# All three convolutions of a conv block as sixteen 32x32 TensorE tiles in two alternating image layouts, with halo rows copied by DMA, one ring of eight PSUM banks, and 16-bit quantising

## The chip, the cores and the metric

The kernel runs on one core of a Trainium2 chip. The metric is the device time of one execution in microseconds, from the first to the last instruction of the slowest core and what little lies around them; lower is better. TensorE is called PE here, VectorE DVE, ScalarE ACT, GpSimd POOL and SyncE SP, as in the profile.

## What is computed

```python
x = x + conv0(gn(x))          # x: 8 images x 32 channels x 128 x 128, f32
x = x + disco(gn(x))          # the output

def conv0(v):                 # 3x3, 32 -> 32 channels, quantised per tensor
    qx = clip(round(v * (127 / max|v|)))      # max over all 8 images
    qw = clip(round(w * (127 / max|w|)))
    return conv3x3(qx, qw) * (max|v| * max|w| / 127**2) + bias

def disco(v):                 # two 3x3 convolutions whose corner taps are zero
    h = lrelu(instnorm(conv5(v, w1)), 0.2)
    return lrelu(instnorm(conv5(h, w2)), 0.2)
```

`gn` is a group normalisation (16 groups of two channels), `instnorm` normalises each channel of each image. The 3x3 kernels of `conv5` are summed from 36 given planes; only the middle and its four neighbours are not zero, so it has five taps where `conv0` has nine. The convolutions are named 0, 1 and 2 below; conv 0 is in f16, conv 1 and 2 are in f32.

## The kernel before

**Layout.** An image stands in SBUF as 128 partitions x 4096 columns. The four groups of 32 partitions are the four parities (row even or odd, column even or odd) of the pixels of each channel, so a group holds a 64x64 image, and a tap either stays in a group or reads another group at a shift of one. Input and output come in this layout by the host's reshaping. The eight images, 2 MB each, stay in `xs` for the whole kernel.

**Matmuls.** One PSUM bank holds 512 columns: eight rows of 64 for all four parities. Convs 1 and 2 use tiles of 64x32: 64 input partitions, 32 output ones, eight tiles of the array (`half_taps`, lines 980 and 986), 32 matmuls for two banks. Conv 0 uses 128x32 tiles (line 1039) for images 0 to 2, and 64x32 ones (`taps0`, lines 1057 and 1064) from image 3 on, which need a copy of the image with its upper and lower partitions exchanged (`qturn`, by DMA, line 304). An image and convolution is four units of two banks. PSUM is a ring of three units (`SLOTS`), and two banks for the small gathers.

**The prologue.** SP loads the images two at a time. DVE and ACT take the statistics of every image, POOL writes the normalised one (line 586), DVE takes its maximum (line 762), and POOL reduces the maxima over the partitions (line 601). Then scale and shift of the quantising are known for all images (line 799, `quant_known`).

**The main part.** Every engine's order is written out by hand, and semaphores connect them. PE goes through `ORDER`: (0,0), (0,1), then for t = 0 to 5 conv 1 of image t, conv 0 of t+2, conv 2 of t, and at last (1,6), (1,7), (2,6), (2,7). What follows a unit:

- conv 0: DVE adds the scaled sum onto x in `xs` (`x1_unit`, line 811) and takes statistics of that (line 817); POOL makes scale and shift of them (`normalise`, lines 554 to 566), ACT writes the normalised image (`make_a`, line 409), the input of conv 1.
- conv 1 and 2: DVE takes statistics in PSUM (`conv_stats`, line 827), ACT copies the unit out (`take`, line 396), and after POOL's `normalise` ACT applies the leaky ReLU (`make_h`, line 419, or `norm_out`, line 428). DVE adds the result of conv 2 and the bias onto x (`output`, line 844), and SP stores it (line 312).
- POOL quantises image t+3 in pieces (`quantise`): scale and shift to f32 (line 634), + 12582912 (line 637), - 12582912 to f16 (line 642).

In each normalisation a matmul of 128x128 on PE (`gather`, line 944) sums the statistics over the partitions that belong together, between DVE's `spread` and `group_moments`.

Of the kernel before, what the change touches and what calls it, by code (L numbers as in the profile page):

```python
# [8 lines left out]
I32 = mybir.dt.int32  # L9
# [8 lines left out]
BLK = IMG // 2  # L18
COLS = BLK * BLK
PAD = BLK + 2  # L20
BANK = 512
BANKS = COLS // BANK
ROWS = BANK // BLK
UNITS = 4
UBANKS = 2
UCOLS = UBANKS * BANK
UROWS = UBANKS * ROWS
SLOTS = 3
EDGES = [0, UROWS + 1, 2 * UROWS + 1, 3 * UROWS + 1, BLK]
QCOLS = (UROWS + 1) * BLK  # L30
TAPS = 9
# [4 lines left out]
KEEP_Q, KEEP_A, KEEP_H = 40, 60, 60  # L36
# [9 lines left out]
GN_ORDER = [0, 1, 2, 3, 4, 5, 6, 7]  # L46

# [36 lines left out]
def conv_block_kernel(nc, x_d, w0_d, bias_d, w12_d, const_d, out_d):  # L84
    psi = disco_psi()
    with ExitStack() as ctx:
# [3 lines left out]
        def sem(name):  # L90
# [3 lines left out]

        xs = sb("xs", [P, B * COLS], F32)
        apad = [sb(f"apad{p}", [P, PAD, PAD], F32) for p in range(2)]
        hpad = sb("hpad", [P, PAD, PAD], F32)
        qpad = sb("qpad", [P, PAD, PAD], F16)
        qturn = sb("qturn", [P, PAD, PAD], F16)
        scaled = sb("scaled", [P, QCOLS], F32)  # L100


        q_one = apad[1][:].rearrange("p r c -> p (r c)").bitcast(F16)[:, 0:PAD * PAD].rearrange("p (r c) -> p r c", c=PAD)
        h_last = xs[:, 0:PAD * PAD].rearrange("p (r c) -> p r c", c=PAD)
        a_last = xs[:, 2 * COLS:2 * COLS + PAD * PAD].rearrange("p (r c) -> p r c", c=PAD)
        own0 = sb("own0", [P, 2, 2, C], F16)
        side0 = sb("side0", [P, 2, 2, C], F16)
        vert0 = sb("vert0", [P, 2, 2, C], F16)
        corn0 = sb("corn0", [P, 2, 2, C], F16)
        turn0 = sb("turn0", [P, 2, 2, C], F16)  # L110
        own12 = sb("own12", [P, 2, 2, 2, C], F32)
        side12 = sb("side12", [P, 2, 2, 2, C], F32)
        vert12 = sb("vert12", [P, 2, 2, 2, C], F32)
        const = sb("const", [P, 2 * P + 3 * (GN_MEMBERS + IN_MEMBERS)], F32)
        single = sb("single", [P, 11], F32)
        bias, minus_half, wmax, wmax_all, wmul, amax1, sx, sx_inv, qmul, dequant, centre = (
            single[:, n:n + 1] for n in range(11))
# [18 lines left out]
        kern = scaled[0:C, 0:2 * TAPS * C].rearrange("p (v k o) -> p v k o", v=2, k=TAPS)  # L136
        kern0 = scaled[0:C, 2 * TAPS * C:].bitcast(F16)[:, 0:TAPS * C].rearrange("p (k o) -> p k o", o=C)
# [5 lines left out]


        stage_at = (B - 1) * COLS

        def staged(cols):
            nonlocal stage_at
            v = xs[:, stage_at:stage_at + cols]
# [3 lines left out]
        w0 = staged(TAPS * C)[0:C]  # L153
        w0_s = staged(TAPS * C)[0:C]
# [3 lines left out]
        gathered_gn = ctx.enter_context(nc.psum_tensor("gathered_gn", [P, BANK], F32))  # L158
        gathered_in = ctx.enter_context(nc.psum_tensor("gathered_in", [P, BANK], F32))
        gather_ps = {s: (gathered_gn if s in ("x", "x1") else gathered_in)[:, at:at + 3 * members[s]]  # L160
                     for s, at in (("x", 0), ("x1", 0), ("c1", 0), ("c2", BANK // 2))}
# [6 lines left out]
        x_in = [sem(f"x_in{b}") for b in range(B)]  # L168
        w0_step = sem("w0_step")
# [5 lines left out]
        weights0_ready = sem("weights0_ready")  # L175
# [43 lines left out]
        def xs_cols(b, c0, n):  # L219
            return xs[:, b * COLS + c0:b * COLS + c0 + n]  # L220

        def xs_rows(b, r0, r1):
            return xs_cols(b, r0 * BLK, (r1 - r0) * BLK)

# [946 lines left out]
```

## Time and profile before

| | |
|---|---|
| times of 3 runs | 382.07, 382.15, 382.69 us |
| the profiled execution | span 381.1 us from first to last instruction |
| PE, DVE, ACT, POOL busy | 76%, 73%, 62%, 44% of the span |
| 0 to 77 us | the prologue, PE almost idle |
| 97 to 361 us | the convolutions, PE always busy but for the gaps of handing over |
| granted TensorE clock, mean | 0.986 |

The profiled execution's own time is not given apart from its span; the median of the runs is 1.05 us above the span. Busy time of PE is the union of matmuls that run side by side, so it says little of how many tiles are at work.

### The profile page before, as it was taken

How to read it: one execution, taken by the hardware profiler on the slowest of the kernel's cores; microseconds unless marked ns; L12 is line 12 of the kernel's file. 1: busy time of each engine (PE TensorE's matmuls, PEld its weight loads, DVE VectorE, ACT ScalarE, POOL GpSimd, SP SyncE). 2: the span in 40 equal slices, each digit the busy share in tenths (PEclk: the TensorE clock that was granted, in tenths of full speed). 3: DMA queues.
4: the chain of work that ended last, by engine and by line, in shares of the span. 5: the costliest groups of instructions: out<-in, count | busy, mean ns of one | idle time of the engine just before them, and what ended most of it. 6: DMA issues, size and time to landing. Idle time of an engine off the chain costs nothing.

```text
span 381.1 us, 12247 instructions
## 1 busy us (share of the span) xinstructions
PE 291.4 (76%) x5544; PEld 119.8 (31%) x5544; DVE 278.6 (73%) x421; ACT 234.9 (62%) x247; POOL 168.3 (44%) x248
## 2 busy tenths in 40 slices
PE   0000100197999999999999999999999999999950
PEld 0000100153334334434433343344334333333310
DVE  3837899879966957885796779678957877444585
ACT  1069998295534585478628753864686379857554
POOL 0189895328948722772396059407921001100110
PEclk9999999999999999999999999999999999999995
DMA  7999700000000042224224302520252202300055
GB/s 264 383 427 425 313 1 1 0 2 2 2 3 2 16 103 114 85 57 100 103 113 93 131 9 113 115 114 32 83 115 114 114 2 83 142 2 2 3 220 220
DMA packets 4978, 40.21 MB, mean 106 GB/s; under 512 B 768, under 2 KB 928, under 8 KB 1440
## 3 DMA queue, kind: packets, MB, share of 16 engines
q1 hardware_dynamic: 4928, 39.45, 28.3%
q8 instruction: 43, 0.70, 0.8%
q14 instruction: 7, 0.06, 0.0%
HBM read 17.26 MB, written 16.78 MB: 89 GB/s over the span
## 4 chain that ended last, share of the span: by engine, by line
PE 54%; DVE 27%; ACT 6%; POOL 6%; issue 3%; DMA 3%; SPq 0%; DVEq 0%; POOLq 0%
PE ring L980 43%; DVE amax L762 8%; DVE xs L844 5%; DVE bn_c L827 4%; PE ring L986 3%; DVE xs L811 3%; DVE bn_x L817 3%; PE ring L1057 3%; DMA xs<-w_dram 3%; PE ring L1039 2%; POOL apad L586 2%; ACT hpad L419 2%; PE gathered_in L944 1%; ACT apad L396 1%; ACT hpad L396 1%
## 5 line engine op out<-in xcount | busy, mean ns | idle before, releaser
L827 DVE BATCH_NORM_STATS2 bn_c<-ring 128x6 f32<-128x512 f32 x128 | 82.1, 687 | 43.4 <-PE ring L986 43.4
L554 POOL TENSOR_SCALAR var_eps<-moments_c 128x1 f32<-128x1 f32 x16 | 3.0, 190 | 145.0 <-DVE moments_c L735 145.0
L396 ACT COPY apad<-ring 128x1024 f32<-128x1024 f32 x28 | 28.3, 1012 | 54.1 <-DVE bn_c L827 54.0
L980 PE MATMUL ring<-hpad,own 64*32 64x512 f32 x448 | 59.2, 591 | 2.9 <-ACT apad L396 1.7
L980 PE MATMUL ring<-hpad,vert 64*32 64x512 f32 x448 | 58.9, 587 | 0.0
L986 PE MATMUL ring<-hpad,own 64*32 64x512 f32 x448 | 58.6, 592 | 0.0
L986 PE MATMUL ring<-apad,own 64*32 64x512 f32 x448 | 58.6, 591 | 0.0
L980 PE MATMUL ring<-apad,own 64*32 64x512 f32 x448 | 58.5, 591 | 0.0
L986 PE MATMUL ring<-apad,side 64*32 64x512 f32 x448 | 58.2, 587 | 0.0
L986 PE MATMUL ring<-hpad,side 64*32 64x512 f32 x448 | 58.1, 587 | 0.0
L980 PE MATMUL ring<-apad,vert 64*32 64x512 f32 x448 | 58.1, 587 | 0.0
L811 DVE SCALAR_TENSOR_TENSOR xs<-ring,single,xs 128x1024 f32<-128x1024 f32 x32 | 39.7, 1268 | 9.7 <-PE ring L1064 8.4
L396 ACT COPY hpad<-ring 128x1024 f32<-128x1024 f32 x28 | 28.4, 1013 | 23.8 <-DVE bn_c L827 23.8
L419 ACT ACTIVATE hpad<-hpad,params 128x1024 f32<-128x1024 f32 (+2 forms) x28 | 32.7, 1234 | 12.3 <-POOL params L566 12.3
L817 DVE BATCH_NORM_STATS2 bn_x<-xs 128x6 f32<-128x512 f32 x64 | 39.8, 677 | 0.0
L428 ACT ACTIVATE apad<-apad,params 128x1024 f32<-128x1024 f32 x28 | 34.0, 1241 | 8.0 <-POOL params L566 8.0
L634 POOL TENSOR_SCALAR scaled<-xs,q_scale,q_shift 128x1024 f32<-128x1024 f32 (+2 forms) x24 | 37.4, 1556 | 1.8
L409 ACT ACTIVATE apad<-xs,params 128x1024 f32<-128x1024 f32 (+2 forms) x28 | 33.2, 1239 | 4.7 <-POOL params L563 4.7
L844 DVE SCALAR_TENSOR_TENSOR xs<-apad,single,xs 128x1024 f32<-128x1024 f32 x28 | 35.1, 1273 | 0.0
L762 DVE TENSOR_REDUCE amax<-apad 128x1 f32<-128x4096 f32 (+1 forms) x7 | 26.3, 3789 | 7.7 <-POOL apad L586 7.7
L642 POOL TENSOR_SCALAR qpad<-scaled 128x1024 f16<-128x1024 f32 (+2 forms) x24 | 25.2, 1048 | 8.9 <-PE ring L1064 7.1
L347 ACT ACTIVATE qpad<-xs 128x4096 f16<-128x4096 f32 x5 | 18.0, 3608 | 17.9 <-DMA xs<-x_dram 17.9
(154 smaller groups left out, 640.6 us busy)
## 6 DMA issues: line engine op xcount, KB each, us to landing
xs<-x_dram SPq DMA_DIRECT2D x8, 2048.0 KB, 9.8
out_dram<-xs SPq DMA_DIRECT2D x14, 1024.0 KB, 3.9
qturn<-qpad SPq DMA_DIRECT2D x10, 528.0 KB, 6.2
out_dram<-xs SPq DMA_DIRECT2D x4, 512.0 KB, 2.8
xs<-w_dram SPq DMA_DIRECT2D x1, 288.0 KB, 9.8
const<-const_dram SPq DMA_DIRECT2D x1, 146.0 KB, 2.4
xs<-w_dram SPq DMA_DIRECT2D x1, 36.0 KB, 1.7
single<-bias_dram SPq DMA_DIRECT2D x1, 0.5 KB, 2.2
```

The lines of the kernel that those rows point to most:

```text
L396: nc.scalar.copy(unit_of(tile, u), grid(slot(v, t, u))).then_inc(taken[v], 1)
L409: nc.scalar.activation(rows_of(a_tile(b), r0, r1), grid(xs_rows(b, r0, r1)), ACT.Identity, bias=param(shift["x1"], b), scale=param(scale[" ...
L419: nc.scalar.activation(rows, rows, ACT.Prelu, bias=param(shift["c1"], t), scale=param(scale["c1"], t), alpha=SLOPE).then_inc(h_ready, 1)
L428: nc.scalar.activation(rows, rows, ACT.Prelu, bias=param(shift["c2"], t), scale=param(scale["c2"], t), alpha=SLOPE).then_inc(out_norm, 1)
L634: nc.gpsimd.tensor_scalar(rows, xs_rows(b, r0, r1), q_scale[:, b:b + 1], q_shift[:, b:b + 1], ALU.mult, ALU.add).then_inc(q_step_pool, 1)
L762: nc.vector.tensor_reduce(amax[:, n:n + 1], gn_tile(b)[:, c0:c1], AX.X, ALU.max, apply_absolute_value=True).then_inc(max_done, 1)
L811: nc.vector.scalar_tensor_tensor(x, slot(0, b, u), dequant[:], x, ALU.mult, ALU.add).then_inc(taken[0], 1)
L817: ins = nc.vector.bn_stats(bn["x1"][:, k, :], xs_cols(b, k * BANK, BANK))
L827: ins = nc.vector.bn_stats(bn[s][:, u * UBANKS + h, :], ring_of(v, t, u)[:, h, :])
L844: nc.vector.scalar_tensor_tensor(x, unit_of(a_tile(t), u), bias[:], x, ALU.add, ALU.add).then_inc(out_ready, 1)
L980: nc.tensor.matmul(bank_out(t, u, v, hp, C * (2 * px + py), C), wv[q0:q0 + 64, v - 1, px, py, :], window(tile, u * UBANKS + hp, dy, 0, q0, ...
L986: ins = nc.tensor.matmul(bank_out(t, u, v, hx, C * (2 * px + py), C), ws[q0:q0 + 64, v - 1, px, py, :], window(tile, u * UBANKS + hx, 0, d ...
```

## The change

**Layout.** The four groups of 32 partitions are now four bands of 32 rows of the image, 128 columns wide (`xa_dram`, the input of conv 0), or four sets of chunks: chunk n of eight rows of every band (`xb_dram`, everything from conv 0's output on; `to_chunks` is the exchange of band and chunk). A matmul takes 32 input partitions (band r) and writes 32 output partitions (c) in bank r, so conv 0 turns bands into chunks, conv 1 turns chunks back into bands, and conv 2 bands into chunks. Hence x is needed in both layouts, and is loaded twice: `load_xb` overwrites the image in `xs` once it has been quantised, and `load_again` brings images 6 and 7, for which `xs` (seven images now) has no room.

**Halos.** Rows above and below a band or chunk lie in other partitions. SP copies them with two DMAs per image for conv 0 and conv 2 (`band_halo`) and four for conv 1 (`a_edges`), of rows of 512 bytes. PE waits for them ahead of its fourth tap.

**Ring.** All eight banks are one ring of two sets of four: half g of a convolution is four banks, and PE waits for half g of the convolution before it to be taken. The gathers go into a bank of a set that has been read.

**Bias.** It was added in `output`; now ACT (image 0) and POOL (`add_bias`) add it onto the reloaded x.

**Quantising.** `low` is a 16-bit integer tile: one operation rounds by its type, the second converts to f16. The exchange copy `qturn` is gone. The last addition (`output`) is POOL's for images 0 to 5 and DVE's for 6 and 7.

```diff
-        apad = [sb(f"apad{p}", [P, PAD, PAD], F32) for p in range(2)]
-        hpad = sb("hpad", [P, PAD, PAD], F32)
+        apad = [sb(f"apad{p}", [P, QUADS, CHUNK + 2, PITCH], F32) for p in range(2)]
+        hpad = [sb(f"hpad{p}", [P, BAND + 2, PITCH], F32) for p in range(2)]
+        low = sb("low", [P, COLS], I16)
-        ring = ctx.enter_context(nc.psum_tensor("ring", [P, SLOTS, UBANKS, BANK], F32))
+        ring = ctx.enter_context(nc.psum_tensor("ring", [P, BANKS, BANK], F32))
@@ PE
+ORDER = [(0, 0), (0, 1), (1, 0)]
+for _t in range(B - 2):
+    ORDER += [(0, _t + 2), (1, _t + 1), (2, _t)]
+ORDER += [(1, B - 1), (2, B - 2), (2, B - 1)]
-                        nc.tensor.matmul(bank_out(t, u, v, hp, C * (2 * px + py), C), wv[q0:q0 + 64, v - 1, px, py, :],
-                                         window(tile, u * UBANKS + hp, dy, 0, q0, 64), start=start, stop=stop)
+            def half(v, b, g):
+                if i > 0:
+                    v0, b0 = ORDER[i - 1]
+                    wait_pairs(v0, b0, g, 2)
+                    wait_moments(GATHERS.get((v, b, 0) if g else (v0, b0, 1), ()))
+                taps = TAPS9 if v == 0 else TAPS5
+                for k, (dy, dx) in enumerate(taps):
+                    if g == 0 and k in (0, 3):
+                        wait_input(v, b, k)
+                    for c in range(QUADS):
+                        for r in range(QUADS):
...
+                            ins = nc.tensor.matmul(ring[C * c:C * (c + 1), QUADS * g + r, :]...,
+                                w, window(v, b, r, c, g, dy, dx),
+                                start=k == 0, stop=k == len(taps) - 1)
@@ SP
+            def load_xb(b):
+                if b == 0:
+                    sp.wait_ge(low_act, 2)
+                sp.wait_ge(low_pool, low_pool_count(b, 4) if b else 2)
+                sp.dma_start(x1_of(b), xb_d[b, :, :]).then_inc(xb_in[b], 16)
+            for t in range(B - 2):
+                if t + 3 < B:
+                    load_xb(t + 3)
+                h_edges(t)
+                if t + 3 < B:
+                    q_edges(t + 3)
+                if t >= 1:
+                    store(t - 1)
+                if t in (1, 2):
+                    load_again(t + 5)
+                a_edges(t + 2)
@@ POOL, ahead of the first conv 0
+            pool.wait_ge(max_done, B + 1)
+            zero_bands(q_one).then_inc(q_border, 1)
+            pool.wait_ge(quant_known, 1)
+            for n in (3, 2):
+                to_low(0, n)
+            for n in (0, 3, 1, 2):
+                to_low(1, n)
@@ POOL, a period
+            def to_low(b, n):
+                nc.gpsimd.tensor_scalar(piece(low_of(b), n), piece(source, n), q_scale[:, b:b + 1], q_shift[:, b:b + 1],
+                                        ALU.mult, ALU.add).then_inc(low_pool, 1)
+            def to_q(b, n):
+                nc.gpsimd.tensor_scalar(bands(qpad)[...], piece(low_of(b), n)..., 1.0, 0.0,
+                                        ALU.mult, ALU.add).then_inc(q_pool, 1)
+            def add_bias(b):
+                    nc.gpsimd.tensor_scalar(x, x, 1.0, bias[:], ALU.mult, ALU.add).then_inc(biased_pool, 1)
+            def output(t, n):
+                pool.wait_ge(out_norm, QUADS * t + n + 1)
+                nc.gpsimd.tensor_tensor(x, x, piece(c2_of(t), n), ALU.add).then_inc(out_pool, 1)
@@ ACT, a period (t >= 1)
+                    take(2, t - 1, 1, 0)
+                    make_a(t + 1, 2)
+                    take(2, t - 1, 1, 1)
+                for n in range(3):
+                    make_h(t, n)
+                    for n in range(QUADS):
+                        norm_out(t - 1, n)
+                for g in range(2):
+                    take(1, t + 1, g, 0)
+                    take(1, t + 1, g, 1)
+                take(2, t, 0, 0)
+                make_a(t + 2, 0)
+                take(2, t, 0, 1)
+                make_a(t + 2, 1)
```

Before, POOL's queue holds this between `normalise` of conv 1 of one image and the next `normalise`, which is that of conv 2 (`scaled` and `qpad` are the quantised image's pieces):

```order
L554 TENSOR_SCALAR var_eps<-moments_c 128x1
L557 TENSOR_TENSOR params<-var_eps,single 128x1
L566 TENSOR_SCALAR params<-moments_c,params 128x1
L634 TENSOR_SCALAR scaled<-xs,q_scale,q_shift 128x1088
L637 TENSOR_SCALAR scaled<-scaled 128x1088
L642 TENSOR_SCALAR qpad<-scaled 128x17x64
```

Three more pieces of the same three operations follow there. Now one period of POOL's queue, from the end of `normalise` of conv 1 (`add_bias` on `xs`, then `low`, `qpad`, and `xs<-xs` for `output`):

```order
L643 TENSOR_SCALAR xs<-xs,single 128x2048 x2
L628 TENSOR_SCALAR low<-xs,q_scale,q_shift 128x1024 x4
L572 TENSOR_SCALAR var_eps<-moments_c 128x1
L575 TENSOR_TENSOR params<-var_eps,single 128x1
L577 TENSOR_SCALAR params<-moments_c,params 128x1
L635 TENSOR_SCALAR qpad<-low 128x8x128 x4
L648 TENSOR_TENSOR xs<-xs 128x1024 x3
L572 TENSOR_SCALAR var_eps<-moments_x 128x1
L575 TENSOR_TENSOR params<-var_eps,single 128x1
L577 TENSOR_SCALAR params<-moments_x,params 128x1
L648 TENSOR_TENSOR xs<-xs 128x1024
```

The twelve quantising operations of a period became eight, and two additions of 2048 columns and four of 1024 columns with two inputs have come in; all three `normalise` stand behind some of them.

Ahead of the first conv 0, from the reduction over partitions on, POOL's queue held this before (`apad` is zeroed at its border, then conv 0's image 1 is rounded; `ISA` are instructions of POOL's own, here the change of its configuration):

```order
L601 ISA single<-single 128x1
L604 MEMSET apad 128x66
L605 MEMSET apad 128x66
L606 MEMSET apad 128x64
L607 MEMSET apad 128x64
L604 MEMSET apad 128x66
L605 MEMSET apad 128x66
L606 MEMSET apad 128x64
L607 MEMSET apad 128x64
L615 ISA
L615 TENSOR_SCALAR hpad<-hpad 128x1088
```

And now:

```order
L612 ISA single<-single 128x1
L615 MEMSET apad 128x2x130
L616 MEMSET apad 128x32x2
L628 ISA
L628 TENSOR_SCALAR hpad<-xs,q_scale,q_shift 128x1024 x6
```

The first arithmetic of POOL behind the change of configuration was work for image 1; it is now work for image 0, the first that PE waits for.

## Rows read from the trace of the kernel before

**Rows 1.** The page, its first row

```profile
span 381.1 us, 12247 instructions
```

**Rows 2.** Busy time by engine (PE, PEld, DVE, ACT, POOL), one period

```profile
188.26:223.59 35.33, 34.64 (x710) 13.88 (x711) 26.97 (x43) 21.76 (x21) 18.46 (x23) 1.00 0.30 93
```

**Rows 3.** Chain that ended last, start and length, where it leaves PE

```profile
192.21 2.40 DVE xs L844 x2
```

**Rows 4.** Timeline of PE: start, length, line, count

```profile
178.98 0.61 PE L980 MATMUL ring<-apad,own 64*32 64x512 f32 x4
179.41 0.61 PE L980 MATMUL ring<-apad,own 64*32 64x512 f32 x4
...
182.42 0.40 PE L1057 MATMUL ring<-qpad,own 64*32 64x512 f16 x4
182.44 0.41 PE L1064 MATMUL ring<-qpad,own 64*32 64x512 f16 x4
182.64 0.40 PE L1057 MATMUL ring<-qpad,vert 64*32 64x512 f16 x4
...
184.53 0.39 PE L1057 MATMUL ring<-qturn,turn 64*32 64x512 f16 x4
...
185.18 0.40 PE L1057 MATMUL ring<-qpad,own 64*32 64x512 f16 x4
```

**Rows 5.** Timeline of DVE in one period

```profile
185.41 3.83 DVE L811 SCALAR_TENSOR_TENSOR xs<-ring,single,xs 128x1024 f32<-128x1024 f32 x3
...
202.54 2.49 DVE L827 BATCH_NORM_STATS2 bn_c<-ring 128x6 f32<-128x512 f32 x4
```

**Rows 6.** Timeline of ACT in the same period

```profile
186.81 4.65 ACT L419 ACTIVATE hpad<-hpad,params 128x1088 f32<-128x1088 f32 x4 [1.74 <-POOL params L566]
...
203.86 1.02 ACT L396 COPY apad<-ring 128x1024 f32<-128x1024 f32 x1
```

**Rows 7.** Timeline of POOL in the same period

```profile
192.19 3.32 POOL L634 TENSOR_SCALAR scaled<-xs,q_scale,q_shift 128x1024 f32<-128x1024 f32 x1
...
197.87 1.20 POOL L634 TENSOR_SCALAR scaled<-xs,q_scale,q_shift 128x1024 f32<-128x1024 f32 x1
199.14 1.04 POOL L637 TENSOR_SCALAR scaled<-scaled 128x1024 f32<-128x1024 f32 x1
200.27 1.05 POOL L642 TENSOR_SCALAR qpad<-scaled 128x1024 f16<-128x1024 f32 x1
...
207.58 0.19 POOL L554 TENSOR_SCALAR var_eps<-moments_c 128x1 f32<-128x1 f32 x1 [2.86 <-DVE moments_c L735]
```

**Rows 8.** Groups by line and form: busy us, mean ns

```profile
L537 POOL TENSOR_TENSOR xs<-xs 32x64 f32<-32x64 f32 x6 | 1.8, 313 | 0.1
...
L586 POOL TENSOR_SCALAR apad<-xs,gn_scale,gn_shift 128x2048 f32<-128x2048 f32 x1 | 2.0, 2048 | 0.1
```

**Rows 9.** POOL and ACT after POOL's second reduction over partitions

```profile
L615 POOLq MODIFY_POOL_CONFIG  x2: 95/95/95, 76.6 to 76.7; - x2
...
84.25 1.09 POOL L615 TENSOR_SCALAR hpad<-hpad 128x1088 f32<-128x1088 f32 x1 [7.45 <-ACT hpad L386]
...
81.42 4.63 ACT L386 ACTIVATE hpad<-xs,q_shift,q_scale 128x1088 f32<-128x1088 f32 x4
```

**Rows 10.** DMA issues: size each, median us to landing

```profile
xs<-x_dram SPq DMA_DIRECT2D x8, 2048.0 KB, 9.8
out_dram<-xs SPq DMA_DIRECT2D x14, 1024.0 KB, 3.9
```

**Rows 11.** Chain that ended last, from the quantising to conv 1

```profile
76.87 4.65 ACT hpad L378 x4
...
96.98 0.56 PE ring L980 x4
```

**Rows 12.** Timeline of DVE, its last instructions

```profile
372.81 4.87 DVE L844 SCALAR_TENSOR_TENSOR xs<-xs,single 128x1024 f32<-128x1024 f32 x4 [2.59 <-ACT xs L428]
```

**Rows 13.** Busy time and granted clock near the end

```profile
370.00:372.00 2.00, 0.00 (x0) 0.00 (x0) 0.21 (x1) 0.46 (x1) 1.00 (x3) 0.67 0.48 197
```

More of the change, by code:

```diff
@@ L168, in conv_block_kernel @@
         x_in = [sem(f"x_in{b}") for b in range(B)]
+        x_in_again = {b: sem(f"x_in_again{b}") for b in (6, 7)}
+        xb_in = [sem(f"xb_in{b}") for b in range(B)]
         w0_step = sem("w0_step")
@@ new lines, in _ @@
+            t, z = B - 2, B - 1
+            take(2, t - 1, 1, 0)
+            make_a(z, 2)
+            take(2, t - 1, 1, 1)
+            for n in range(3):
+                make_h(t, n)
+            take(1, z, 0, 0)
+            take(1, z, 0, 1)
+            for n in range(QUADS):
+                norm_out(t - 1, n)
+            take(1, z, 1, 0)
+            take(1, z, 1, 1)
+            for n in range(3):
+                make_h(z, n)
+            for g in range(2):
+                take(2, t, g, 0)
+                take(2, t, g, 1)
@@ L511, in _ @@
+            take(2, z, 0, 0)
+            take(2, z, 0, 1)
+            for n in range(QUADS):
+                norm_out(t, n)
+            take(2, z, 1, 0)
+            take(2, z, 1, 1)
+            for n in range(QUADS):
+                norm_out(z, n)
         @block.gpsimd
@@ L662, in _ @@
+            add_bias(1)
+            normalise("x1", 0, GN_EPS)
+            for n in range(4):
+                to_low(2, n)
+            for n in range(4):
+                to_q(2, n)
+            pool.wait_ge(conv_done[0], 4)
+            zero_chunks(apad[1]).then_inc(a_border, 1)
+            add_bias(2)
+            normalise("x1", 1, GN_EPS)
+            normalise("c1", 0, IN_EPS)
             for t in range(B - 2):
+                more = t + 3 < B
+                if more:
+                    for n in range(4):
+                        to_low(t + 3, n)
@@ L677, in _ @@
-            norm_c(2, B - 3)
-            norm_x1(B - 1)
-            norm_c(1, B - 2)
-            norm_c(1, B - 1)
-            norm_c(2, B - 2)
-            norm_c(2, B - 1)
+                    normalise("c2", t - 1, IN_EPS)
+                if more:
+                    for n in range(4):
+                        to_q(t + 3, n)
+                if t >= 1:
+                    for n in range(3):
+                        output(t - 1, n)
+                normalise("x1", t + 2, GN_EPS)
+                if t >= 1:
+                    output(t - 1, 3)
@@ L933, in _, with output @@
-            x1_stats(1, 3)
-            spread_stats("x1", 1)
-            for t in range(B - 2):
-                period(t)
-            last_periods()
+            def output(t, n):
+                dve.wait_ge(out_norm, QUADS * t + n + 1)
+                x = piece(x1_of(t), n)
+                nc.vector.tensor_tensor(x, x, piece(c2_of(t), n), ALU.add).then_inc(out_dve, 1)
+            for n in (0, 3, 1, 2):
+                to_q(0, n)
+            for n in (0, 3, 1, 2):
+                to_q(1, n)
```

1042 lines of the change are left out of this document (434 added, 608 removed).

## The prediction

> **What bounds the kernel now.** I read the busy time of one period first (conv 2 of one image to conv 2 of the next): 35.33 us, PE busy for 34.64, DVE 26.97, ACT 21.76, POOL 18.46 [rows 2]. The chain of waits stays on PE but for one detour a period, where a PSUM unit is late because DVE does two `output` additions (2.40 us) ahead of its statistics [rows 3]. So PE bounds the main part. The timeline of PE says why: eight f32 records start every 0.43 us and eight f16 ones every 0.22 us [rows 4]; an f32 matmul is two records. Convs 1 and 2 are 128 matmuls each, 256 records, 32 rounds, 13.8 us; conv 0 is 24 rounds, 5.3 us; a gather spreads two rounds from 0.22 to 0.65 us [rows 4], so costs 0.43. 2 x 13.8 + 5.3 + 3 x 0.43 = 34.2, the period.
>
> **The change on PE.** Sixteen records a round instead of eight, if the round keeps its length. Conv 1 or 2: 5 taps x 2 halves x 2 records = 20 rounds, 8.6 us. Conv 0: 9 x 2 = 18 rounds, 4.0 us. With three gathers the period is 2 x 8.6 + 4.0 + 1.3 = **22.5 us** of PE. Eight starts lie within a few hundredths of a microsecond (182.42 and 182.44 for two groups of four [rows 4]), so issue has room for sixteen in 0.22. The Trainium skill, "TensorEngine Tiling (Array Packing)", Instruction Overhead, speaks against that: it gives about 60 cycles for each matmul. At 2.4 GHz that would be an estimated 0.40 us for sixteen, so conv 0 would take 7.2 us and PE 25.7 a period, f32 unchanged. The trace disagrees: two groups of four start 0.02 us apart.
>
> **DVE.** 24 statistics at 0.61 us (2.49 for four) and four additions from PSUM at 1.25 (3.83 for three) [rows 5] stay; the four SBUF additions of 1.20 [rows 3] leave. 26.97 - 4.8 = **22.1 us**. **ACT** keeps its eight copies of 1.0 and its three times 4096 columns of 4.65 us or a little less [rows 6]: **21.6 us**.
>
> **POOL** gets the work, added up over its new period (starts of neighbours in [rows 7] include the gap):
> - four `to_low` at 1.27 = 5.1 (two per-partition operands; 197.87 to 199.14), four `to_q` at 1.13 = 4.5 (1.05 and the gap). f16 output costs what f32 costs (1.05, 1.04), so I give 16-bit integers the same.
> - two `add_bias` of 2048 columns at 2.1 (2.05 [rows 8]) = 4.2.
> - three `normalise` of 1.3 = 3.9 (the first starts at 207.58, three operations and what wakes them).
> - four `output` with two SBUF inputs, 1024 columns. No row has that. Below: the one-input 1.05. Above: 313 ns for 64 columns [rows 8] against 190 ns for one column [rows 7] is 1.95 ns a column, 2.2 us; with the same growth that one-input operations show at length (about a fifth), 2.6. I take 2.35 with the gap, the middle of the upper two, as the two-input row is the nearer one: 9.4.
>
> Sum **27.1 us**. The Trainium skill, "GPSIMD Engine Reference", Performance versus the Vector engine, has 4497 ns for a two-input addition of 2048 columns; halved, an estimate of 2.25, it would leave the sum where it is. No row of this case shows it.
>
> So POOL, not PE, sets the period: 27.1 against 35.3. I walked one period with these prices through all queues, time 0 being the end of POOL's `normalise` of conv 1. POOL: bias to 4.2, `to_low` 9.3, c2 10.6, `to_q` 15.1, three outputs 22.2, x1 23.5, output 25.9, c1 27.2. The others arrive ahead of it: x1's gather is through at 20.6 and c1's at 24.5, ACT's `norm_out` waits for c2 and runs 10.6 to 15.3, and so PE's conv 2 starts only at 17.2, when ACT has taken conv 1. Slack is 1.4 to 1.6 us. PE idles 3.2 us between the halves of conv 0, whose bank set ACT empties late, because `make_a` stands between two takes. Halo DMAs go out behind 2 MB loads on SP (at 9.3, landing by about 17; PE wants them at 19.8), hidden.
>
> **The start gets longer.** Now: quantising known at 76.87, conv 1 of image 0 starts at 96.98 [rows 11]. In the changed kernel:
> - POOL's configuration changes after its reduction over partitions. MODIFY_POOL_CONFIG is at 76.6, and POOL's next arithmetic starts at 84.25, though its data from ACT was there at 82.7 [rows 9]: 7.5 us. That was hidden behind image 0; now POOL must make half of image 0 first. With two memsets ahead of it instead of eight I put the change at 76.0, + 7.5 = 83.5; two pieces to 86.1; a cast on DVE, conv 0 starts 86.5.
> - Only then may x be loaded again: 86.2 + 6.9 = 93.1. (2 MB alone is between twice what 1 MB needs, less one latency of about 1, so 6.8, and the 9.8 of two in flight [rows 10].) ACT adds the bias, 4.7: 97.8.
> - DVE adds and counts both halves, 99.0 to 106.8, and one more addition for image 1, to free the bank of the gather: 108.0. Gather, group, POOL 1.3: 110.8. `make_a`, two pieces: **113.6**, conv 1 of image 0. That is 16.6 us later than before.
> - The pipe fills: `add_bias` of image 2 (load, then 4.2) holds `normalise` of image 1 to 128.4; ACT's takes stand behind `make_a` of image 1, so the second half of conv 0 of image 2 starts at 133.1. Then 2.5 (conv 0), 8.6 (conv 1), 8.2 to c1's gather in conv 2, 1.3: end of the first c1 `normalise` in the loop at **153.7**.
>
> **Periods.** Four to the one of the last loop: 153.7 + 4 x 27.1 = 262.1.
>
> **The end.** conv 1 of image 6 from 269.3 (7.3 later), conv 2 of image 5 from 277.9, conv 1 of image 7 from 288.8, conv 2 of image 6 from 299.1, which stops about 3.3 us because ACT does `norm_out` of image 5 ahead of a take. POOL's four outputs of image 5 end at 310.5, and c1's last `normalise` stands behind them: 311.7. `make_h` and takes to 318.1; conv 2 of image 7, 8.2, to 326.3; DVE's statistics stand behind outputs of image 6 and end at 334.3; spread, gather, last piece, POOL: 337.6; ACT and DVE as today's last 4.87 us with their start (1.24 earlier, [rows 12]): 343.5. From DVE's last end today (377.7 [rows 12]) to the span's (381.1 [rows 1]) are 3.4 us: 346.9.
>
> I add 2 us for some forty hand-overs of 0.05 us that the walk left out: span 349. The median is 1.05 us above the span today: **350 us**.
>
> **The rivals.**
> - *A, the forecast*: POOL bounds at about 27; 344 to 357 us. 0.50.
> - *B, POOL adds as fast as with one input.* Then POOL needs 22.2, and the walk is bound by the loop of PE, DVE and ACT at 25.5: five periods at 1.6 less and 4.2 less at the end: 338 us. For it: one-input operations lie near one column a nanosecond. Against: 313 against 190 ns. 0.17.
> - *C, PE is slower than its rounds.* Its idle stretches of 1 to 3 us could bring the granted clock to the lower level, 1.2 GHz. For it: in 370 to 372 us PE does nothing and the granted clock falls to 0.67 [rows 13]. Against: the gaps are shorter than that. If half a conv 0 and some of conv 1 run at half speed, PE takes 3 us more a period, 1.5 beyond the slack, and 4 more in start and end: 361 us. The same price holds for the 60 cycles. The Trainium skill, "TensorE: Matmul & The Clock Gate", also says that idle stretches between bursts bring the clock down. 0.16.
> - *D, 16-bit integers are slow on POOL*, the other side. If writing and reading them costs what a second input costs (2.4 us for 1024), eight operations a period are 9.6 us more, POOL needs 36.7, above today's 35.3, over six images 57 us: 410 us. It decides from (382 - 350) / 48 = 0.67 us more an operation, 1.9 us. Against: the f16 row. 0.07.
> - *E, the change doesn't do what it says:* sixteen tiles take turns, a round being 0.86 us. PE needs 2 x 17.2 + 8 + 1.3 = 43.7 a period: about 480 us. From 0.7 us a round it is slower than now. Against: rounds of eight last exactly their 1024 columns. 0.03.
> - *F, the configuration is there in time*, say because the 7.5 us had another cause: 343 us. 0.07.
>
> That POOL is held up by DVE (3.32 for 1.20 us beside the two SBUF additions [rows 3, 7]) mostly goes away, since DVE keeps only additions from PSUM beside it; it is no rival.
>
> **The numbers.** A, B, C and F hold 0.90; the range 337 to 368 takes in B's lower end, C, a second input at 2.6 (6 us more) and the reload at 9.8. Faster by over 0.2% (about what a measurement here can tell from no change) 0.89, within 0.2% 0.01, slower 0.10.
>
> **What would show it.** Steps: PE records of 16 within 0.43 and 0.22 us; `output` on POOL near 2.3 us; POOL busy over nine tenths of a period of 27 us; its first `to_low` near 83.5; conv 1 of image 0 near 114; last c1 `normalise` right behind four outputs. Wrong if POOL idles in a period, if rounds are longer, or if halo DMAs are what PE waits for.

## The result and the profile after

| | median us | fast to slow | ratio to before, 95% |
|---|---|---|---|
| before, beside it | 382.42 | 382.07 to 385.79 | |
| changed | 410.77 | 408.44 to 415.67 | 1.070, 1.063 to 1.078 |
| forecast | 350.0 | 337 to 368 | |

The change makes the kernel slower by 7%. The profiled execution of the changed kernel took 415.67 us, the longest of its four (granted clock 0.885, where the three shorter ones had 0.895 to 0.903), so single times below run a few us high.

The page of the changed kernel, its first lines (span, busy time, slices of a fortieth of the span):

```profile
span 413.9 us, 16194 instructions
...
PE 258.0 (62%) x7528; PEld 152.5 (37%) x7528; DVE 249.5 (60%) x379; ACT 218.6 (53%) x185; POOL 216.0 (52%) x238
...
PE   0010100443577789799569977998797899619920
...
POOL 0298966092384441993956396379735630630000
PEclk9999999958669899899958977999899999956965
```

PE is no longer busy all through the main part [rows 1, 2], its clock falls several times, and POOL, which was to be the bound, works half of the span. Two stretches, each from a `normalise` of conv 1 to another, from the windows: four periods of the changed kernel, and three of e15 below:

```profile
core 0: us, PE busy (x) PEld busy (x) DVE busy (x) ACT busy (x) POOL busy (x), PEclk, DMA share, GB/s
165.42:310.69 145.27, 123.75 (x3753) 72.98 (x3748) 89.00 (x148) 84.12 (x73) 100.05 (x93) 0.89 0.48 164
```

```profile
187.17:280.23 93.06, 82.59 (x2819) 53.04 (x2814) 70.48 (x111) 63.47 (x55) 75.01 (x70) 1.00 0.27 94
```

A period is 145.27 / 4 = 36.3 us where 27.1 was forecast and 35.3 stood before [rows 2]. POOL is busy for 25.0 of it (forecast 27.1 with the gaps), DVE 22.3 (22.1), ACT 21.0 (21.6). So three engines have about the prices that the prediction gave them. PE has not, and it waits besides.

**Rounds.** The timeline of PE, taps of sixteen tiles at the full clock (clock 1.00 from 253.7 to 294.6): 160 f32 records between two gathers, and 80 f16 records ahead of one, to be held against [rows 4].

```profile
268.96 5.54 PE L979 MATMUL ring<-hpad,w12t 32*32 32x512 f32 x160
274.44 0.39 PE L917 MATMUL ring<-spread_c,const 128*128 128x12 f32 x2
...
282.01 1.36 PE L979 MATMUL ring<-qpad,w0t 32*32 32x512 f16 x80 [1.28 <-ACT xs L442]
283.30 0.39 PE L917 MATMUL ring<-spread_c,const 128*128 128x12 f32 x2
```

From start to start, sixteen f32 records take 5.48 / 10 = 0.55 us, not 0.43; sixteen f16 ones 1.29 / 5 = 0.26, not 0.22. So conv 1 or 2, 20 rounds, is 11.0 us and not 8.6, and conv 0, 18 rounds, is 4.6 and not 4.0. With three gathers of 0.32 (274.44 to 274.76) PE needs 27.5 us a period, 5 more than forecast.

**Stops.** The period that begins at 198.7 us, PE's timeline (start, length, and idle time ahead of it in brackets):

```profile
198.89 1.43 PE L979 MATMUL ring<-qpad,w0t 32*32 32x512 f16 x67
201.56 1.32 PE L979 MATMUL ring<-qpad,w0t 32*32 32x512 f16 x76 [1.25 <-issue]
204.18 1.04 PE L979 MATMUL ring<-qpad,w0t 32*32 32x512 f16 x52 [1.29 <-ACT xs L442]
209.68 1.07 PE L979 MATMUL ring<-qpad,w0t 32*32 32x512 f16 x28 [4.45 <-issue]
...
212.89 2.76 PE L979 MATMUL ring<-apad,w12t 32*32 32x512 f32 x33
216.09 10.92 PE L979 MATMUL ring<-apad,w12t 32*32 32x512 f32 x279 [0.43 <-issue]
```

"issue" means that the profile shows nothing that held PE. It stops in the middle of a tap, for 4.45 us. What the DMA queues did meanwhile, in two windows, 204.9 to 207.1 and 207.1 to 208.3 us:

```profile
## 3 DMA queue, kind: packets, MB, share of 16 engines
q1 hardware_dynamic: 102, 0.59, 83.5%
```

```profile
q1 hardware_dynamic: 560, 0.30, 107.6%
q8 instruction: 1, 0.02, 5.1%
```

The data queue fills the DMA engines (a 2 MB read, the halo copies, and soon another read), and queue 8 has no packet until 207.19. That one lands at 208.16, and PE goes on at 209.68. The packet itself is not slow (0.97 us; the median between 120 and 350 us is 1.10, and 1.03 in the kernel before); it starts late, 2.0 us after PE has stopped. When it was asked for, the trace does not show. A packet of queue 8 is 16 KB, and PE has 15056 instructions on 59 packets, so one packet is some 255 instructions (128 matmul records). Counting PE's instructions, fifteen stops between 120 and 350 us (0.8 to 4.8 us from start to start) lie 254 to 256 instructions apart or at multiples of that, and each ends 1.2 to 1.6 us after such a packet has landed. So PE waited for its own instructions. It eats a packet in 8 x 0.26 = 2.1 us in conv 0 and 4.4 in the f32 convs; with eight tiles it was 3.5 and 6.9. An estimate from these numbers: a packet's own 0.9 us and the 1.2 behind it already make the 2.1 in which conv 0 uses one up, so there is little to spare there even on idle DMA engines.

The clock, in windows of the same stretch (columns as above):

```profile
204.00:206.00 2.00, 1.04 (x52) 0.62 (x53) 2.00 (x4) 2.00 (x3) 2.00 (x3) 0.97 1.05 360
206.00:219.00 13.00, 8.89 (x184) 4.20 (x192) 4.49 (x7) 7.03 (x6) 7.85 (x9) 0.50 0.75 234
```

From 206 us, within the stop of 4.45 us, to 219 TensorE has 1.2 GHz, and conv 1 lasts 13.6 us. Not only stops at instructions do this. One period later PE waits for ACT's copy between the halves of conv 0, the gap that the prediction put at 3.2 us, and the clock is at 1.2 GHz behind it (0.50 from 243.9 to 246.8 us):

```profile
243.94 2.36 PE L979 MATMUL ring<-qpad,w0t 32*32 32x512 f16 x80 [2.88 <-ACT xs L442]
```

**The end.** The chain of waits:

```profile
356.93 9.30 POOL xs L648 x4
366.23 0.02 issue
366.24 0.34 SPq L358
366.58 0.04 issue
366.63 0.56 SPq L317
367.19 0.04 issue
367.23 3.64 DMA hpad<-hpad
370.87 0.14 issue
371.00 4.08 PE ring L979 x64
```

SP sends h's halo rows of image 6 behind its store of image 5 (L358), and that store waits for POOL's four outputs. PE idles 11.5 us. The walk followed PE, DVE, ACT and POOL here, and not SP.

**The start and POOL** came out close to the forecast: 82.64 for the first `to_low` (83.5), 7 us behind the change of configuration; conv 1 of image 0 starts at 115.97 (113.6); `output` takes 2368 ns (2.35 with the gap), 16-bit integers cost nothing extra in the loop (1197 ns; the six operations at the start took longer, 8.55 us together).

```profile
82.64 8.55 POOL L628 TENSOR_SCALAR hpad<-xs,q_scale,q_shift 128x1024 int16<-128x1024 f32 x6 [6.88 <-issue]
```

```profile
115.97 9.68 PE L979 MATMUL ring<-apad,w12t 32*32 32x512 f32 x222 [3.15 <-ACT apad L451]
```

```profile
L648 POOL TENSOR_TENSOR xs<-xs 128x1024 f32<-128x1024 f32 x24 | 56.3, 2368 | 2.7 <-ACT xs L468 2.7
...
L628 POOL TENSOR_SCALAR low<-xs,q_scale,q_shift 128x1024 int16<-128x1024 f32 x24 | 28.4, 1197 | 0.0
L635 POOL TENSOR_SCALAR qpad<-low 128x1024 f16<-128x1024 int16 x24 | 24.5, 1049 | 3.9 <-PE ring L979 3.9
```

### The profile page after: what moved, and what is told of

Same layout as the page of the kernel before. It is cut to its first block, busy times and chain, and to the rows that moved or that the text cites. A ratio compares the mean times of both kernels' runs of the same rounds, so it can differ in the third digit from the quotient of the medians.

```text
span 413.9 us, 16194 instructions
## 1 busy us (share of the span) xinstructions
PE 258.0 (62%) x7528; PEld 152.5 (37%) x7528; DVE 249.5 (60%) x379; ACT 218.6 (53%) x185; POOL 216.0 (52%) x238
## 4 chain that ended last, share of the span: by engine, by line
PE 44%; DVE 17%; issue 10%; POOL 10%; ACT 8%; DMA 8%; SPq 1%; DVEq 0%; POOLq 0%; ACTq 0%
PE ring L979 42%; DVE amax L759 7%; DMA xs<-xb_dram 4%; ACT xs L442 3%; DVE bn_c L832 2%; DMA hpad<-w_dram 2%; POOL xs L648 2%; DVE xs L847 2%; PE ring L917 2%; POOL apad L597 2%; ACT hpad L460 2%; DVE xs L817 1%; DVE bn_c L739 1%; DVE bn_x L824 1%; ACT apad L451 1%
## 5 line engine op out<-in xcount | busy, mean ns | idle before, releaser
L979 PE MATMUL ring<-hpad,w12t 32*32 32x512 f32 x2560 | 99.8, 621 | 14.4 <-DMA hpad<-hpad 11.5
L979 PE MATMUL ring<-apad,w12t 32*32 32x512 f32 x2560 | 98.9, 644 | 10.1 <-issue 6.3
L979 PEld LDWEIGHTS ring<-apad,w12t 32*32 32x32 f32 x2560 | 54.2, 107 | 48.2 <-issue 33.3
L979 PE MATMUL ring<-qpad,w0t 32*32 32x512 f16 x2016 | 45.9, 452 | 33.1 <-issue 12.4
L979 PEld LDWEIGHTS ring<-hpad,w12t 32*32 32x32 f32 x2560 | 49.7, 104 | 45.6 <-issue 31.3
L648 POOL TENSOR_TENSOR xs<-xs 128x1024 f32<-128x1024 f32 x24 | 56.3, 2368 | 2.7 <-ACT xs L468 2.7
L442 ACT COPY xs<-ring 128x1024 f32<-128x1024 f32 x32 | 32.1, 1006 | 38.1 <-DVE bn_c L832 38.1
L451 ACT ACTIVATE apad<-xs,params 128x1536 f32<-128x1536 f32 (+1 forms) x24 | 36.6, 1534 | 18.4 <-POOL params L577 18.4
L460 ACT ACTIVATE hpad<-hpad,params 128x1536 f32<-128x1536 f32 (+1 forms) x24 | 35.0, 1530 | 17.7 <-POOL params L577 17.7
L468 ACT ACTIVATE xs<-xs,params 128x1024 f32<-128x1024 f32 x32 | 37.1, 1230 | 9.5 <-POOL params L577 9.4
L628 POOL TENSOR_SCALAR low<-xs,q_scale,q_shift 128x1024 int16<-128x1024 f32 x24 | 28.4, 1197 | 0.0
L635 POOL TENSOR_SCALAR qpad<-low 128x1024 f16<-128x1024 int16 x24 | 24.5, 1049 | 3.9 <-PE ring L979 3.9
```

The lines of the kernel that those rows point to most:

```text
L442: nc.scalar.copy(halves(c2_of(t), g, pair), got).then_inc(taken[2], 1)
L451: nc.scalar.activation(chunks(apad[b % 2])[:, :, ROW_SETS[n], :], rows4(x1_of(b))[:, :, ROW_SETS[n], :], ACT.Identity, bias=param(shift["x ...
L460: nc.scalar.activation(rows, rows, ACT.Prelu, bias=param(shift["c1"], t), scale=param(scale["c1"], t), alpha=SLOPE).then_inc(h_ready, 1)
L468: nc.scalar.activation(y, y, ACT.Prelu, bias=param(shift["c2"], t), scale=param(scale["c2"], t), alpha=SLOPE).then_inc(out_norm, 1)
L628: nc.gpsimd.tensor_scalar(piece(low_of(b), n), piece(source, n), q_scale[:, b:b + 1], q_shift[:, b:b + 1], ALU.mult, ALU.add).then_inc(low ...
L648: nc.gpsimd.tensor_tensor(x, x, piece(c2_of(t), n), ALU.add).then_inc(out_pool, 1)
```

## The experiments

Theory I: PE needs 27.5 us a period by its rounds, and its instruction fetches starve beside the x reads, which also brings the clock down. Rival H: halo transfers hold PE. Rival K: the order of ACT's copies makes a gap between the halves of conv 0, and the gap the low clock; DMA traffic doesn't matter. All ratios are to the kernel before on the same chip, which had 383.2 to 384.0 us there; the changed kernel had 1.070. How long PE idles at "issue" differs between executions of the same loop: between 120 and 350 us it is 21.1 us in the changed kernel's trace, 21.3 in e1's and 14.7 in e2's, whose loop is the changed kernel's. A difference of a few microseconds between two traces is therefore no finding.

**e1, the tiles in diagonals.** 411.0 us, 1.070 (1.065 to 1.076).

```diff
-                    for c in range(QUADS):
+                    for d in range(QUADS):
                         for r in range(QUADS):
+                            c = (r + d) % QUADS
```

> Sixteen matmuls of a tap go in diagonals: neighbours in the order differ in their row group and in their column group. In the changed kernel sixteen f32 records take 0.54 us at the full granted clock (160 records in 5.4 us), not the 0.43 of the kernel before, and sixteen f16 ones 0.25. Theory of the order (neighbours that share a column group hold each other up): f32 falls to about 0.43, PE needs some 4 us less a period, the kernel 20 to 28 us less than the changed kernel, 380 to 390. Theory of issue (sixteen small matmuls with their weight loads take that long to hand over, in any order): 0.54 stays, the time within 2 us of the changed kernel.

Nothing changes. That neighbours in the order share a column group is not what makes 0.55 us.

**e5, eight tiles of sixteen in three of five taps.** 391.76 us, one run.

```diff
+                            if 0 < k < 4 and (v == 1 and r > 1 or v == 2 and c > 1):
+                                continue
```

> The changed kernel, but in the taps 2 to 4 of conv 1 only row groups 0 and 1 and in those of conv 2 only column groups 0 and 1 are multiplied (eight tiles of sixteen; the values of conv 1 and 2 are then wrong). It measures what a tap of sixteen f32 records costs when there are only eight tiles. Issue theory (handing over 16 f32 records with their weight loads takes 0.54 us whatever they do): a tap of eight tiles is bound by its columns, 0.43 a record round, 0.86 a tap; the three taps take 2.6 us a half instead of 3.2. Load theory (each tile's weight load of 0.1 us is not hidden behind its own matmul): 0.54 stays with eight tiles, 3.2 us. If only one of the two forms speeds up, row or column groups are what is shared.

Between the same two gathers of conv 2, which hold two taps of sixteen tiles and three of eight:

```profile
252.14 5.00 PE L981 MATMUL ring<-hpad,w12t 32*32 32x512 f32 x112
257.06 0.39 PE L917 MATMUL ring<-spread_c,const 128*128 128x12 f32 x2
```

4.92 us, less two taps of 1.10, leaves 0.91 for a tap of eight tiles, close to twice 0.43, against 1.10 for sixteen. So eight 32x32 tiles run at nearly the speed of their columns, and the second eight cost 0.19 us more instead of nothing. That speaks against a weight load that each tile pays for itself. It fits a limit in handing over, 1.10 us / 32 = 34 ns a record, but does not show one: an f16 record of the same 512 columns takes 16 ns, so it is not one time for every record, and a limit on the data that sixteen tiles move at once would fit as well. Matmuls of fewer columns would tell the two apart; none was run.

**e2, halo ahead of the store.** 404.6 us, 1.056 (1.050 to 1.061).

```diff
-            store(B - 3)
             h_edges(B - 2)
+            store(B - 3)
```

> Only the end changes: SP issues the halo DMAs of h of image 6 before it waits for the output of image 5, no longer behind it. PE's 11.5 us idle at the halo should go. Theory of the queue on SP: 8 to 11 us less than the changed kernel, 400 to 403, and the clock stays up for the first half of conv 2 of image 6. Rival (the DMA itself is late, or ACT's copies behind norm_out hold PE anyway): 3 us less or nothing.

The 11.5 us are gone, but only about 6 are gained, less than expected. PE now waits 5.7 us one convolution later, for ACT's copies of conv 2 of image 6 (L442):

```profile
366.43 10.89 PE L979 MATMUL ring<-hpad,w12t 32*32 32x512 f32 x256 [5.71 <-ACT xs L442]
```

The copies stand behind `make_h` of image 7, whose `normalise` stands behind POOL's four outputs. That wait was in the forecast; it had only been covered.

**e3, no 2 MB reads in the loop.** 393.0 us, 1.023 (1.019 to 1.028).

```diff
-                    load_xb(t + 3)
-                if t in (1, 2):
-                    load_again(t + 5)
```

> Leaves out the 2 MB reads of the loop: x for the bias and shortcut of images 3 to 7, and x again for images 6 and 7, so their values are stale; halo DMAs, stores and all arithmetic stay. Theory I (PE's instructions, 16 KB a fetch, come too late beside the 2 MB reads): the stops of PE of 0.6 to 4.5 us that lie 256 PE instructions apart go or fall under 0.3 us, and with them the low clock of 206 to 219 us; 15 to 25 us less than the changed kernel, near 390. Rival K (order of ACT's copies and the f32 rounds make the periods, DMA traffic does not matter): within 4 us of the changed kernel, the stops stay.

17 to 18 us less, as theory I said; K falls. The stops do not go entirely, though, as theory I wanted. Groups by line, conv 1 and conv 0 of e3:

```profile
L974 PE MATMUL ring<-apad,w12t 32*32 32x512 f32 x2560 | 91.0, 613 | 5.6 <-ACT apad L447 3.8 <-issue 1.9
...
L974 PE MATMUL ring<-qpad,w0t 32*32 32x512 f16 x2016 | 47.8, 473 | 26.4 <-ACT xs L438 7.8 <-DVE qpad L801 7.7 <-issue 5.3
```

and of the changed kernel:

```profile
L979 PE MATMUL ring<-apad,w12t 32*32 32x512 f32 x2560 | 98.9, 644 | 10.1 <-issue 6.3
...
L979 PE MATMUL ring<-qpad,w0t 32*32 32x512 f16 x2016 | 45.9, 452 | 33.1 <-issue 12.4
```

"issue" falls from 18.7 to 7.2 us over both, and six stops of up to 1.7 us are left. The granted clock of the four periods is 0.93 where it was 0.89: it still falls behind the gaps that wait for ACT. The period is 31.8 us instead of 36.3.

**e4, no halo DMAs.** 397.5 us, 1.034 (1.030 to 1.039).

```diff
-                band_halo(q_of(b), q_halo[b % 2])
-                        pe.wait_ge(q_halo[b % 2], 32 * (b // 2 + 1))
```

(and the same for a and h)

> Leaves out all halo DMAs and PE's waits for them, so the rows at band edges are stale; the 2 MB reads and stores stay. Theory I: the stops stay, since they come from the 2 MB reads; the end gains what the halo wait cost, 9 to 12 us: 398 to 402. Theory H (small halo transfers, landing in up to 10 us, hold PE or crowd the queues): stops go in the loop too, 20 to 30 us less.

7 us beyond e2. The stops stay, but shorter (2.3 us for the one of 4.8, "issue" 11.3 over both groups). Against e2, the nearer comparison, that stop is 2.3 instead of 2.9 and "issue" between 120 and 350 us 10.3 instead of 14.7; besides, PE's wait of 2.3 us for a halo ahead of the loop is gone. So the halo traffic adds to the crowd at most and is not its cause; H holds for a part.

**e6, each read as four of 1024 columns.** 419.4 us, 1.096 (1.091 to 1.100).

> Each 2 MB read of the main part is issued as four reads of 1024 columns, 4 KB a packet and not 16 KB; same bytes. Theory I, with the size of the packets ahead of the 16 KB instruction fetch as what delays it: stops at 256 instructions shrink, 5 to 12 us less than the changed kernel. Theory I, with the bytes as what counts: within 4 us of the changed kernel.

Worse by 9 to 10, which neither theory expected. Small packets don't let the fetches through; a stop of 5.1 us came out. Why more packets are worse was not measured apart.

**e7, both copies ahead of `make_a`** (shown for one half of conv 2, done for both), and **e8, sixteen matmuls of 256 columns that fill the gap.** 408.5 us, 1.066 (1.064 to 1.069), and 409.2 us, 1.069 (1.066 to 1.072).

```diff
                     take(2, t - 1, 1, 0)
-                    make_a(t + 1, 2)
                     take(2, t - 1, 1, 1)
+                    make_a(t + 1, 2)
```

> ACT does both copies of a half of conv 2 ahead of make_a, not one on each side of it. Theory K (this order makes the gap of about 3 us between the halves of conv 0, and the gap the low clock after it): PE's wait for ACT there falls from 1.2-3 us to under 0.5, 1.5 us a period and some half-speed stretches, 8 to 15 us less than the changed kernel. Theory I (instruction fetches take over whatever time that gives): 0 to 4 us less, the stops at 256 instructions get longer.

> The changed kernel with 16 more matmuls of 256 columns (about 1.7 us) in PE's gap between the halves of conv 0, into a bank that is free; no change in who waits for whom, and 8 KB more instructions a period. It separates the clock from the gap: if the low clock after this gap costs time, the stretches at 1.2 GHz that begin there go and the kernel gains 3 to 12 us; if the stops at instruction fetches bring the clock down, it stays and the kernel is 0 to 6 us slower than the changed kernel.

The same place as above, in e7 and in e8:

```profile
202.70 1.05 PE L979 MATMUL ring<-qpad,w0t 32*32 32x512 f16 x52
208.39 1.07 PE L979 MATMUL ring<-qpad,w0t 32*32 32x512 f16 x28 [4.65 <-issue]
```

```profile
200.17 1.36 PE L984 MATMUL ring<-qpad,w0t 32*32 32x512 f16 x80 [0.54 <-ACT xs L442]
...
205.96 0.65 PE L984 MATMUL ring<-qpad,w0t 32*32 32x512 f16 x14 [3.15 <-issue]
```

PE arrives earlier and stops all the same. And the clock of 120 to 350 us, of e8 and of the changed kernel:

```profile
120.00:350.00 230.00, 206.72 (x6356) 124.42 (x6346) 144.31 (x244) 138.51 (x119) 137.80 (x137) 0.99 0.41 140
```

```profile
120.00:350.00 230.00, 197.03 (x6043) 116.21 (x6049) 140.20 (x237) 131.73 (x113) 135.83 (x133) 0.92 0.41 140
```

e8 restores the clock from 0.92 to 0.99 here (over whole executions it is 0.912 to 0.921 against 0.885 to 0.903) and gains nothing that can be told from the spread, which would hide about 3 us. It also hands PE 192 more instructions, one packet (32 or 2 KB a period, not the 8 KB expected). So while the supply of instructions sets the pace, neither the gap nor the clock was shown to cost more than a few microseconds by itself; a price of the clock of that size is not excluded.

**e9, the reads paced by SP.** 419.8 us, 1.095 (1.090 to 1.099).

```diff
+                for n in range(QUADS):
+                    if n and b > 2:
+                        sp.wait_ge(xb_in[b], 16 * n)
+                    sp.dma_start(piece(x1_of(b), n), piece(xb_d[b, :, :], n)).then_inc(xb_in[b], 16)
```

(and the same for x again)

> The 2 MB reads of the loop are issued in four pieces of 512 KB, each only when the one before has landed, so that at most 512 KB stand in the queues; SP is held up some 3 us longer by it. Theory I in the form that the backlog of queued data is what an instruction fetch waits behind: stops 256 instructions apart fall under about 1 us each, 8 to 18 us less than the changed kernel. If they stay at 1.5 to 5 us, the bytes on the DMA engines count, not the backlog, and the time is the changed kernel's or some us more (SP's other transfers come later).

"issue" before PE is at most 1.2 us at a time now, and 4.6 us instead of 21.1 between 120 and 350 us. That speaks for the backlog in the queues as what a fetch waits behind; part of it may be that PE stands still elsewhere meanwhile. For SP waits for each piece to land, and sends the halos later, and the kernel is 9 to 10 us slower where 8 to 18 less were expected:

```profile
162.58 8.11 PE L985 MATMUL ring<-hpad,w12t 32*32 32x512 f32 x160 [6.79 <-DMA hpad<-hpad]
...
222.25 6.22 PE L985 MATMUL ring<-apad,w12t 32*32 32x512 f32 x130 [5.39 <-DMA apad<-apad]
```

**e10, e2 and e7 and ACT making all of image 0's 16-bit x**; **e11, with the pacing of e9.** 395.5 us, 1.030 (1.025 to 1.035), and 405.7, 1.059 (1.054 to 1.064).

> Three repairs together: halo DMAs ahead of the store at the end (404.6 alone), ACT's copies of a half next to each other, and ACT making all four pieces of image 0's 16-bit x, which POOL can start only after its configuration. The last should bring the first x read and conv 1 of image 0 forward by about 5 us. Expected: 5 to 6 us less than the halo repair alone, 397 to 401, still slower than the kernel before, as the f32 rounds of 0.54 us and the stops stay.

> The three repairs and the paced reads. If pacing removes the stops, what it gained alone comes on top, 382 to 390, near the kernel before; otherwise as without pacing.

In e10 conv 1 of image 0 starts at 110.1 instead of 116.0. e11 confirms e9 and misses its 382 to 390: on SP the pacing costs 10 us more than it brings.

**e12, e10 with ACT issuing the reads in pieces; e14, the same from `norm_out` on, with e13's end.** In both, the reads of images 6 and 7 again stay on SP, but behind conv 1's halos and paced. e12 reads behind the second copy of each half of conv 1, behind conv 2's second copy and behind the next `make_a`; e14 reads here:

```diff
+                read(t + 3, 0)
                 for g in range(2):
                     take(1, t + 1, g, 0)
+                    if g == 0:
+                        read(t + 3, 1)
                     take(1, t + 1, g, 1)
+                    read(t + 3, 2 + g)
```

> As the three repairs (395.5), but the loop's reads of x for images 3 to 7 are issued by ACT in four pieces spread over conv 1 and 2, away from conv 0, and the reads of images 6 and 7 again are issued behind the halo DMAs of conv 1 and paced. Theory I (a backlog of queued data delays PE's instruction fetches; pacing on SP gained it and lost it again to halos held up on SP): no stop at an instruction fetch over 1 us, no halo wait over 1 us, 380 to 389. If it stays at 393 or above, pacing costs what it brings.

e12: 402.8 us, 1.053 (1.046 to 1.060), 7 to 9 us more than e10, where 380 to 389 us were expected. The last pieces went out just ahead of conv 0, stops of 4 us stayed there, and POOL had to wait for x:

```profile
POOL xs L653 <- DMA xs<-xb_dram: 41.9, 7, 7.9
```

(41.9 us in all, 7 times, longest 7.9; two of the seven, 10.4 us, lie ahead of the loop). So the place was suspected. Two to four copies earlier (e14), and e13, which is e14 with the reads left on SP:

> The three repairs of e10 (395.5), and at the end: POOL's normalise of conv 1 of image 7 behind two of the four outputs of image 5 instead of four, the copies of conv 2 of image 6 ahead of make_h of image 7, c2 of images 6 and 7 in slots that are free. PE's wait of 6.3 us ahead of conv 2 of image 7 should shrink to 0 to 2: 389 to 392. If something else of the end is late, 394 to 396.

> e13, with the reads of images 3 to 7 issued by ACT in four pieces from norm_out on (earlier than in e12, where POOL waited 8 us a period for the last piece), and the reads of images 6 and 7 again behind conv 1's halo DMAs, paced. Placing theory: conv 0 is then free of the x read but for images 6 and 7 again, stops over 1.5 us are left in two periods only, 378 to 386. Bytes theory: the stops only move into conv 1, 388 to 394.

e13: 390.8 us, 1.017 (1.011 to 1.024). e14: 381.8 us, 0.996 (0.992 to 1.000). Moving and pacing the reads is worth 9 us. In e14 the clock is 1.00 from 135 to 349 us, "issue" before PE is 2.3 us at most, and 13.8 us in all between 120 and 350 us, where e13 has 20.2. POOL no longer waits for x in the loop.

**e15, e13 without the reads** (x is stale, as in e3). 373.7 us, 0.973 (0.967 to 0.979).

> e13 without the 2 MB reads of the loop, as e3 (x for bias and shortcut of images 3 to 7 and x again for 6 and 7 stale). e3 gained 17 us; the same here gives 372 to 376, the first version below the kernel before, with periods near 29 us: 27.1 of PE at its rounds of 0.54 and 0.25 us and about 2 of waiting between the halves of conv 0. If it ends at 350 to 360, the rounds were not what bounds it.

A period is 31.0 us at the full clock (the second window above), two more than expected. Its timeline shows what stands beside the 27.5 of PE's rounds:

```profile
222.85 1.36 PE L974 MATMUL ring<-qpad,w0t 32*32 32x512 f16 x80 [1.61 <-ACT xs L439]
...
226.35 0.41 PE L974 MATMUL ring<-qpad,w0t 32*32 32x512 f16 x9 [0.82 <-issue]
...
241.74 0.40 PE L912 MATMUL ring<-spread_x,const 128*128 128x24 f32 x2 [1.19 <-ACT hpad L437]
```

ACT's copy between the halves of conv 0 (1.6), a gather that waits for ACT's copy of conv 1 (1.2 to 1.6), and one short stop: 3.6. 27.5 + 3.6 = 31.1.

**e16, e14 with the last halo too ahead of the store.** 379.6 us, 0.985 (0.980 to 0.989).

> e14 (381.8), with SP issuing the halo DMAs of h of image 7 too ahead of the store of image 5. PE's wait of 2.8 us at that halo goes; 379 to 380, a ratio near 0.991. If DVE or ACT hold conv 2 of image 7 anyway, 381 to 382.

The wait of 2.8 us at that halo is gone; a stop at instructions of 2.1 us stands in the same convolution. This version is 1.5% faster than the kernel before, a small gain, but clear of the interval, and 8% faster than the change as it was made (0.985 to 1.070).

## Why the prediction was wrong

The profiled span is 413.9 us, the forecast's 349. By the walk's own marks: the first c1 `normalise` of the loop ends at 165.7 instead of 153.7 (12), the four periods are 36.3 instead of 27.1 (37), and from there to the end it is 103 instead of 87, the 2 us of hand-overs counted in (16). Of the first 12, the start has 2; the rest comes behind it, from longer rounds, stops at instructions and the clock of 1.2 GHz from 137.6 to 141.0 us.

- **The step that failed first: "Sixteen records a round instead of eight, if the round keeps its length."** It rested on two groups of four that start 0.02 us apart [rows 4], taken as proof that issue has room for sixteen. That showed that two groups can start together, and not a sustained rate. A round is 0.55 and 0.26 us, so PE needs 27.5, and with ACT's copies between, 31.1 (e15). "So POOL, not PE, sets the period" fell with it: POOL idles 11 us of 36. The Trainium skill, "TensorEngine Tiling (Array Packing)", Instruction Overhead, warned in the right direction: its 60 cycles a matmul would make 0.40 us for sixteen f16 ones, and measured is 0.26, some 39 cycles each. For f32 it is 34 ns a record, where the prediction kept "f32 unchanged". So rival C had the right engine, and its 3 us a period were too low a price; measured are 5.
- **Nothing in the sum stood for the instructions.** The change cuts the time that 256 of PE's instructions last from 3.5 to 2.1 us in conv 0 and from 6.9 to 4.4 in the others, and raises what the DMA engines move from 40.2 to 61.4 MB: 2 MB of reads and 0.6 MB of halos an image, and 2 MB again for two images, in place of the exchange copies. The prediction called the halos hidden and gave instructions no term, without a reason. The reads cost 17 us as the change stood (e3 against the changed kernel, and e15 against e13), 9 of which come back by moving them (e14).
- **"The gaps are shorter than that"** [rows 13], against rival C, was wrong: the granted clock was 0.50 behind the forecast's own gap for ACT (2.9 us) and behind stops of 1.3 and 4.5 us, and 0.92 from 120 to 350 us. But e8, with 0.99, was no faster beyond the spread.
- **The x read** was put at 6.9 us; it took 8.7 to 10.7. The halos were put at some 8 us to landing and called hidden; they took up to 10 us, and in the loop PE never waited for one. What they add to the stops is within e4's 7 us.
- **The end** missed SP's queue: 11.5 us at one halo, of which 6 counted (e2).
- **Right:** DVE, ACT and POOL by their sums, `output` at 2.35, int16 at no cost (D), the configuration (7 us, against F), that ACT makes a gap between the halves of conv 0 (3.2 us; 1.0 to 3.6 measured), conv 1 of image 0 within 2.4 us, and the last `normalise` behind four outputs (e13, which takes it and the copies around it out of the way, gains 4 to 5 us on e10).
- **A slip in the sum of rival D:** 350 + 57 is 407 and not 410. Nothing hangs on it.

What stays open: what in TensorE limits a record to 34 ns (f32) and 16 ns (f16) with sixteen tiles; e1 and e5 exclude the order of the column groups and a load paid by each tile, no more. Why four times as many packets made fetches worse (e6), and which of pacing, place and issuing engine brings e14's 9 us. And what the low clock costs by itself.

## What to carry to other kernels

Before counting on smaller tiles, take the shortest sustained time per record that the trace shows, not the shortest gap between two, and give it a rival in which it is the bound. Count instructions as traffic: once 256 of PE's instructions last only 2 to 4 us, large reads can hold them up. Here it was worth 9 us to issue them in paced pieces, by a queue that nobody waits behind, away from the stretch that eats instructions fastest; pacing them on SP's queue, which others waited behind, lost as much. And walk SP's queue like an engine: a halo copy behind a store that waits for the slowest engine is a wait for that engine.

## What the runs showed of the hardware that was not expected

- PE's instructions came in packets of 16 KB, one for some 255 instructions, which took 0.9 to 1.5 us themselves; PE resumed 1.2 to 1.6 us after one had landed, and went up to 4.8 us without a matmul when the DMA engines were full.
- Eight 32x32 f32 tiles (all rows, two column groups) run a tap of 512 columns in 0.91 us (e5), sixteen in 1.10; a tap of sixteen f16 tiles takes 0.26.
- The same 2 MB as four reads of 4 KB packets, all issued at once, cost 9 to 10 us more than as one (e6).
- Two-input additions on POOL of 1024 columns take 2368 ns, one-input operations 1049 to 1197, whether f16 or 16-bit integers are written.
